# Layer 0 of a two-layer graph network on one Trainium2 core: seven quads a pair instead of eight, features loaded once

## What is computed

```python
edge_index = jnp.stack([src, dst])
row, col = (edge_index[0], edge_index[1])
tp = fctp_messages(node_features[col], edge_attr_tensor, W1, W2, W3, W4)   # bilinear in node (160) and edge (32) features
messages = tp @ Wm + bm
agg = jax.ops.segment_sum(messages, row, num_segments=N_NODES)
```

## Time and profile before

| | us |
|---|---|
| median of 3 runs (2830.77 to 2832.46) | 2830.84 |
| the profiled execution, its own time | 2835.33 |
| its span in the trace | 2833.5 |
| the message loop in it, first pair to last scatter | 65 to 1295 |
| one chunk in it, rank to rank | 25.05 |

### The profile page before, as it was taken

One profiled execution on the slowest core, in us unless ns is written; L12 is line 12 of the kernel. 1 busy time (PEld: TensorE's weight loads), 2 busy tenths in 40 slices (PEclk: granted clock), 3 DMA queues, 4 the chain that ended last, 5 costly groups with the idle time before them and its releaser, 6 DMA issues. The chain is left out here.

```text
span 2833.5 us, 54044 instructions
## 1 busy us (share of the span) xinstructions
PE 2614.8 (92%) x16778; PEld 2330.6 (82%) x16778; DVE 1979.4 (70%) x5259; ACT 852.2 (30%) x2319; POOL 1662.2 (59%) x1770
## 2 busy tenths in 40 slices
PE   4999999999999999996999968999999999998997
PEld 2888788888888888886999958988888888888886
DVE  7677567766667767663777856766777676667766
ACT  2444344444444444431222212222222222222221
POOL 1666566666666666662100017777777777777775
PEclk8999999999999999998999979999999999999999
DMA  6899999999888999865888845333333333333332
GB/s 232 294 314 314 299 319 316 319 324 320 290 290 287 291 300 294 294 215 187 279 279 280 284 141 149 90 86 88 100 86 90 86 101 88 86 88 99 87 88 68
DMA packets 433880, 584.01 MB, mean 206 GB/s; under 512 B 75752, under 2 KB 372409, under 8 KB 421002
## 3 DMA queue, kind: packets, MB, share of 16 engines
q10 hardware_dynamic: 237795, 282.85, 30.4%
q0 software_dynamic: 84144, 149.09, 17.9%
q1 hardware_dynamic: 111656, 148.48, 16.3%
HBM read 352.08 MB, written 228.11 MB: 205 GB/s over the span
## 5 line engine op out<-in xcount | busy, mean ns | idle before, releaser
L444 POOL DMA_INDIRECT placed<-message,slots_now x784 | 762.9, 973 | 486.5 <-ACT message L613 326.6
L1429 POOL DMA_INDIRECT f_y<-y_table,b_rec x894 | 855.4, 957 | 289.6 <-issue 181.9
L528 PEld LDWEIGHTS g_bank<-quad_ring,front_work 128*128 128x128 f32 x6272 | 878.5, 191 | 98.9 <-issue 96.5
L528 PE MATMUL g_bank<-quad_ring,front_work 128*128 x6272 | 942.1, 304 | 8.0 <-DMA quad_ring<-products 7.5
L772 DVE SCALAR_TENSOR_TENSOR front_work<-g_bank,quarter_node,front_work 128x512 f32<-128x512 f32 x784 | 529.6, 743 | 44.2 <-PE g_bank L505 31.8
L1619 PE MATMUL e_bank<-f_msg,f_hot 128*126 128x160 f32 x1788 | 387.6, 312 | 71.7 <-DVE f_msg L1493 70.6
L1490 DVE TENSOR_TENSOR f_msg<-e_bank,f_y 128x256 f32<-128x256 f32 x447 | 189.2, 423 | 319.7 <-issue 223.9
L1614 PE MATMUL e_bank<-f_msg,f_hot 128*126 128x160 f32 x1788 | 395.8, 303 | 18.0 <-DVE f_msg L1493 15.3
L1619 PEld LDWEIGHTS e_bank<-f_msg,f_hot 128*126 128x126 f32 x1788 | 282.0, 189 | 122.9 <-DVE f_msg L1493 121.4
L1602 PE MATMUL e_bank<-fc,b_hidden 100*128 100x192 f32 x1788 | 372.0, 330 | 0.0
L613 ACT COPY message<-g_bank 128x320 f32<-128x320 f32 x392 | 167.2, 427 | 561.9 <-PE g_bank L528 561.9
(11 more groups left out here) (237 smaller groups left out, 2622.7 us busy)
## 6 DMA issues: line engine op xcount, KB each, us to landing
products<-g ACTq DMA_DIRECT2D x49, 2560.0 KB
quad_ring<-products ACTq DMA_DIRECT2D x98, 1280.0 KB
big<-placed SPq DMA_DIRECT2D x49, 1458.0 KB, 7.1
front_work<-in_e_t SPq DMA_DIRECT2D x392, 64.0 KB
b_lengths<-length_parts ACTq DMA_DIRECT2D x447, 45.0 KB
placed<-zeros SPq DMA_DIRECT2D x24, 648.0 KB
f_y<-y_table,b_rec POOLq DMA_INDIRECT x894
placed<-message,slots_now POOLq DMA_INDIRECT x784
```

The source lines that it names most:

```text
L444: pool.indirect_dma_start(v.placed[:, :], bass.IndirectOffsetOnAxis(slots_now[tile // SET % SLOT_SETS][:, tile % SET:tile % SET + 1], 0), ...
L528: last = pe.matmul(bank_now[:, n * D:n * D + D], spread[batch % SPREADS][:, j, q * P:q * P + P], ring[:, bass.ds(slot + j, 1), :].rearrang ...
L1429: pool.indirect_dma_start(f_y[:, tile % Y_RING, :], None, v.y_table[:, :], bass.IndirectOffsetOnAxis(b_rec[b % REC_RING][:, j, 0:1], 0)).t ...
```

## The change

**A joint quad.** A tile needs its fourth quad only where its last node lies more than 11 above its base. Now each tile has three matmuls of its own, and the pair has one more for the tile of the two that needs a fourth (the first, where neither does): seven instead of eight. Its weights are one 128x128 matrix, its quad and its output column (0 or 160) come from registers. VectorE builds three matrices of 128x512 and two of 128x128 a batch instead of four of 128x512. A pair in which both tiles need a fourth quad is added to the violations.

**Words.** A batch has six entries in `places` instead of four: four words (a tile's place and, 8 bits up, the joint place or column) and, for VectorE, the two numbers that say which tile's edges the joint matrix takes. TensorE takes the words apart in registers; VectorE reads its two once a batch. `positions` is longer by ten small steps.

**Features.** One transfer of 32 partitions a batch instead of two; ScalarE copies three quarters (three copies of 32x512) instead of one half (one of 64x512).

```diff
-                    for n in range(2):
-                        sp.dma_start(features[h][32 * n:32 * n + 32, :, :].rearrange("p a b -> p (a b)"), t["e32_t"][:, edges]).then_inc(edges_in[h], 16)
+                    sp.dma_start(features[h][0:32, :, :].rearrange("p a b -> p (a b)"), t["e32_t"][:, edges]).then_inc(edges_in[h], 16)
...
                     for n in range(2):
                         q = pair % 2 * 2 + n
-                        slot = places[batch][q]
-                        for j in range(WINDOW):
-                            last = pe.matmul(bank_now[:, n * D:n * D + D], spread[batch % SPREADS][:, j, q * P:q * P + P],
-                                             ring[:, bass.ds(slot + j, 1), :].rearrange("p a b -> p (a b)"), start=(j == 0), stop=(j == WINDOW - 1))
-                    last.then_inc(expanded, 1)
+                        slot = nc.s_assert_within(words[batch][q] & (2 ** FIELD - 1), 0, RING_QUADS - 1, skip_runtime_bounds_check_because=OF_RING)
+                        for j in range(WINDOW - 1):
+                            pe.matmul(bank_now[:, n * D:n * D + D], spread[batch % SPREADS][:, j, q * P:q * P + P],
+                                      ring[:, bass.ds(slot + j, 1), :].rearrange("p a b -> p (a b)"), start=(n == 0 and j == 0), stop=False)
+                    m = pair % 2
+                    slot = nc.s_assert_within(words[batch][2 * m] >> FIELD, 0, RING_QUADS + WRAP - 1, skip_runtime_bounds_check_because=OF_RING)
+                    column = nc.s_assert_within(words[batch][2 * m + 1] >> FIELD, 0, D, skip_runtime_bounds_check_because=OF_RING)
+                    pe.matmul(bank_now[:, bass.ds(column, D)], spread[batch % SPREADS][:, WINDOW - 1, m * P:m * P + P],
+                              ring[:, bass.ds(slot, 1), :].rearrange("p a b -> p (a b)"), start=False, stop=True).then_inc(expanded, 1)
...
-                    act.copy(features[h][64:128, :, :], features[h][0:64, :, :]).then_inc(features_doubled, 1)
+                    for n in range(1, 4):
+                        last = act.copy(features[h][32 * n:32 * n + 32, :, :], features[h][0:32, :, :])
+                    last.then_inc(features_spread, 1)
...
-                    for j in range(WINDOW):
-                        last = dve.scalar_tensor_tensor(spread[batch % SPREADS][:, j, :], p_node[h % 2][:], v.quarter_node[:, j:j + 1],
-                                                        features[h].rearrange("p a b -> p (a b)"), ALU.is_equal, ALU.mult)
+                    flat = features[h].rearrange("p a b -> p (a b)")
+                    longer = nc.values_load_multi_w_load_instructions(
+                        v.places[:, ENTRY * batch + BATCH:ENTRY * batch + ENTRY], [mybir.EngineType.DVE], min_val=0, max_val=P,
+                        skip_runtime_bounds_check_because="a tile's first edge in its pair is 0 or P")[1]
+                    for j in range(WINDOW - 1):
+                        dve.scalar_tensor_tensor(spread[batch % SPREADS][:, j, :], p_node[h % 2][:], v.quarter_node[:, j:j + 1], flat, ALU.is_equal, ALU.mult)
+                    for m in range(2):
+                        edges = bass.ds(longer[m] + 2 * P * m, P)
+                        last = dve.scalar_tensor_tensor(spread[batch % SPREADS][:, WINDOW - 1, m * P:m * P + P], p_node[h % 2][:, edges],
+                                                        v.quarter_node[:, WINDOW - 1:WINDOW], flat[:, edges], ALU.is_equal, ALU.mult)
```

More of the change, by code:

```diff
@@ L23 @@
 BATCHES = TILES // BATCH
+ENTRY = 6
+FIELD = 8
 PAIRS = TILES // 2
@@ L182, in build_program @@
         v.quarter_node = sb("quarter_node", [P, WINDOW])
-        v.places = sb("places", [1, TILES], I32)
+        v.places = sb("places", [1, BATCHES * ENTRY], I32)
         v.scattered_order = sb("scattered_order", [1, 1], I32)
@@ L260, in front_phase @@
         excess = sb("excess", [P, 2])
+        entry = sb("entry", [CHUNKS, CHUNK // BATCH, ENTRY], I32)
+        long = sb("long", [CHUNKS, CHUNK])
+        fourth = sb("fourth", [CHUNKS, 4, CHUNK // 2])
         small = sb("small", [CHUNKS, 8, CHUNK])
@@ L460, in _, with load_words @@
             def _(pe):
-                places = {}
-                def load_places(batch):
+                words = {}
+                OF_RING = "a place is a quad between 0 and UNITS * UNIT less the ring's laps before it, a column 0 or D"
+                def load_words(batch):
                     if batch >= BATCHES:
                         return
-                    places[batch] = nc.values_load_multi_w_load_instructions(
-                        v.places[:, BATCH * batch:BATCH * batch + BATCH], [mybir.EngineType.PE], min_val=0, max_val=RING_QUADS - 1,
-                        skip_runtime_bounds_check_because="a place is a quad between 0 and UNITS * UNIT less the ring's laps before it")[1]
+                    words[batch] = nc.values_load_multi_w_load_instructions(
+                        v.places[:, ENTRY * batch:ENTRY * batch + BATCH], [mybir.EngineType.PE], min_val=0, max_val=2 ** 17 - 1,
+                        skip_runtime_bounds_check_because="a word is a place and, FIELD bits up, a place or a column")[1]
                 def unit(b, j):
@@ L501, in spread_ids @@
                     batch, h = pair // 2, pair // 2 % 4
-                    pe.wait_ge(edges_in[h], batch // 4 * 48 + 48)
+                    pe.wait_ge(edges_in[h], batch // 4 * 32 + 32)
                     if batch >= 2:
@@ L519, in expand @@
                     if pair % 2 == 1:
-                        load_places(batch + 1)
+                        load_words(batch + 1)
                     pe.wait_ge(built, batch + 1)
@@ L614, in copy_pair @@
                     if pair % 2 == 1:
-                        double_features(pair // 2 + 4)
+                        spread_features(pair // 2 + 4)
                     if k % 4 == 3:
@@ L629, in _ @@
                 for batch in range(4):
-                    double_features(batch)
+                    spread_features(batch)
                 act.wait_ge(ones_set, 1)
@@ L680, in misfits @@
                     tables.link(dve.tensor_tensor(small[:, 7, :], small[:, 5, :], small[:, 6, :], ALU.add))
+                    of_pair = long[:].rearrange("c (p q) -> c p q", q=2)
+                    tables.link(dve.tensor_tensor(fourth[:, 2, :], of_pair[:, :, 0], of_pair[:, :, 1], ALU.mult))
+                    tables.link(dve.tensor_reduce(fourth[:, 3, 0:1], fourth[:, 2, :], AX.X, ALU.add))
                     tables.link(dve.tensor_reduce(chunk[:, 0:1], small[:, 7, :], AX.X, ALU.add))
+                    tables.link(dve.tensor_tensor(chunk[:, 0:1], chunk[:, 0:1], fourth[:, 3, 0:1], ALU.add))
                 def block_starts():
```

35 lines of the change are left out of this document (26 added, 9 removed).

## The result

The changed kernel takes 2804.4 us in the median of four runs (2802.05 to 2805.29), the kernel before 2830.81: a ratio of 0.9905, 95% interval 0.9893 to 0.9917. It saves 26 us and not 83. The profiled execution took 2805.29 us, its span is 2803.6.

What follows compares the result with a forecast made beforehand. TensorE was taken to set the pace, with the DMA engines nearest behind. Gain 100.1 us less 3.3 (start) and 14 (DMA) is 82.8; off the 2830.84 us median that gives 2748 us, 8-in-10 range 2732 to 2785.

Steps and rivals of the forecast that it cites:

- TensorE, 0.272 us a pair less: Message loop: one matmul (two passes) fewer a pair, 2.18 us a chunk, chunk 22.87 us; extra register instructions cost nothing.
- How many chunks gain: 46 chunks gain 2.18 us each, 100.1 us; the last three gain nothing, GpSimd's scatters end them at 1.275 us steps.
- The start, 3.3 us: Before the loop: VectorE's ten small steps and ScalarE's two more first copies lose 3.3 us, between 1.2 and 5.
- The loads of the words: Register loads in the loop: VectorE's new one 0.3 us a batch, hidden; TensorE's 0.35 us, hidden behind queued matmuls.
- the forecast 3 to 4.5: Sign in the loop: VectorE's wait before `held` falls from 6.55 us a chunk to 3 to 4.5 us.
- The rival that had a register load as bound: VectorE's load at the head of each build sets the pace, kernel slower, up to 2924 us; chance 0.04.
- ScalarE's copies at nothing: Loop: eight more copies a chunk, 4.9 us, covered by ScalarE's 11.8 us of waiting for TensorE; cost nothing.
- The sign that I named: Waits on `copied` or on ScalarE's feature copies would show the ScalarE term, costed at nothing, to be wrong.
- The DMA, 14 us: Ring loads lag shorter chunks: 0.5 us lost in each of the first 25, 0.1 in 21 others; bounds nothing to 62.
- my own test (chunks of both halves equal): Sign: equal chunks in both halves would refute the DMA term, which expected 23.2 to 23.6 us before 800 us, 22.9 after.
- the 10 to 20 that I named as a sign: Sign in the loop: TensorE waits on `quad_ring` 10 to 20 us in all, in place of 7.5.
- Its case, 2734: First rival: the DMA costs nothing more in the loop, so the kernel takes 2734 us; chance 0.15.

Runs made afterwards that it cites:

- aligned_products_first: Changed kernel with eight-word entries, four-word aligned loads, and ScalarE's feature copies behind the products' issue: 2778.6 us, 0.9797 (repeat, `_again`); 1.0108 on the 3199.7 us chip.
- before_new_features: Kernel before with only the features' part: one 64 KB transfer a batch, three 32x512 ScalarE copies; 1.0012 on the 3199.7 us chip, repeat 2836.8 us, 1.0003.

## Why the prediction was wrong

The range ended at 2785; the time is 2804. By its own steps:

- **TensorE, 0.272 us a pair less: right.** With both stalls gone the rank matmuls above are 22.98 and 22.95 us apart (22.87 forecast). So the two more register instructions a pair, costed at nothing, cost about 0.1 us a chunk at most.
- **How many chunks gain: as forecast.** GpSimd ends the phase with its last 48 scatters 1.275 us apart (answer to the earlier trace rows):

```profile
1211.13 0.96 POOL L448 DMA_INDIRECT placed<-message,slots_now  x1 [5.35 <-ACT message L624]
...
1271.06 0.97 POOL L448 DMA_INDIRECT placed<-message,slots_now  x1 [0.30 <-issue]
```

- **The start, 3.3 us: about right.** The matmul of ids after VectorE's first build stands at 68.39 against 64.28, 4.1 us later, and the count that the first rank matmul waits for 1.9 us later (44.24 against 42.35):

```profile
44.24 0.66 PE L499 MATMUL g_bank<-r_count,before 128*128 128x49 f32 x2 [9.84 <-DVE r_count L761]
...
62.91 7.56 ACT L613 COPY front_work<-front_work 32x512 f32<-32x512 f32 x12 [8.55 <-issue]
...
68.39 0.58 PE L510 MATMUL g_bank<-id_rows,ones 1*128 1x512 bf16 x1 [13.96 <-DVE front_work L810]
```

- **The loads of the words: the first step that failed.** I costed VectorE's new load (0.3 us; it takes 0.53, and 1.8 once a chunk) and took TensorE's own at its 0.35 us as before, though the change moves it from 16-byte steps to 24-byte steps. No row of the kernel before has an unaligned load, so its price couldn't be read there; that the load can become long could: it took up to 1.142 us, and its long ones stood once a chunk, right behind an issue of ScalarE. TensorE's load went from 0.93 to 3.7 us there and became a stall of 1.1 us a chunk. VectorE's load is hidden in the main: its wait ahead of `held` is still 4.50 us, at the upper end of the forecast 3 to 4.5 (answer to the earlier trace rows). The rival that had a register load as bound had the wrong engine.

```profile
639.08 0.21 DVE L776 TENSOR_TENSOR held<-held,r_count 128x49 f32<-128x49 f32 x1 [4.50 <-PE g_bank L500]
```

- **ScalarE's copies at nothing: the second.** The sum asked whether ScalarE was busy and whether the pair's message came first. It didn't ask what stood behind the copies: the products' issue, with the odd ring load queued behind it. The copies set that issue back by 1.26 us. The sign that I named, waits on `copied` or on its feature copies, could not show it; a part of the delay comes back 16 us later as a wait for a ring load.
- **The DMA, 14 us: a mechanism half right, and too small.** A ring load "of the second kind" was named with its four pairs, but how near it was to being late was read from 7.5 us of waits in all, not from the 1.6 to 2.1 us to spare that landing times show. By my own test (chunks of both halves equal) the term was not what held the changed kernel. Its 14.7 us of waits on `quad_ring` lie in the 10 to 20 that I named as a sign, but that is luck: they are what the stall behind the load left over, and 54.0 us without it. Once both stalls are gone something of the kind is there: mean chunks of 24.41 and 23.12 us are 1.54 and 0.25 over 22.87, and 1.54 x 25 + 0.25 x 21 = 44 us instead of 14. Some 9 us of it are in the kernel before too, whose mean chunk is 25.42 in the first half, and most of that lies in two chunks: chunks 8 and 9, counted from 0, take 27.3 and 30.1 us there, and 26.0 and 30.6 in aligned_products_first_again. SyncE sends `block_start` at that place (L429, at 282.8 us); whether that is the cause wasn't tried.
- **The sum by the loop's length.** Before, the loop's first to last scatter takes 1223.4 us (the earlier trace rows has its end), after 1196.2: 27.1 less. In aligned_products_first_again it is 1160.6, 62.8 less. So of the 86.1 that I expected of the loop (100.1 - 14), 35.7 went into the two stalls and 23.3 more are missing even without them. I put those beside the DMA term, whose cause stays open.
- **The Trainium skill's rule** ("DMA: Bandwidth & Descriptors", Specifications: some 358 GB/s of HBM for a core) would have made the DMA term nothing. Its case, 2734, didn't come either. The row that I set against it (319 GB/s at a share of 1.00) shows no ceiling though: a window of the changed kernel reaches 399.

```profile
444.00:448.40 4.40, 4.40 (x33) 4.00 (x32) 3.36 (x8) 2.43 (x6) 2.68 (x4) 1.00 1.03 399
```

Another page of the Trainium skill ("HBM Reference", Specifications (TRN2)) says that a core which streams alone gets well above that share; by that, the trace agrees.

## What to carry to other kernels

Cost a change of a table's layout at every engine that reads it into registers: in these runs the cheapest load was one of four words from a multiple of 16 bytes. Of a step that is put on an engine, ask what DMA issue stands behind it, and follow that transfer to the one who needs it; the landing time against the first use gives the slack, which no busy share does. Where taking away one stall brings nothing, look for a second in the same stretch before giving the first one up: the version with aligned entries and the copies behind the products saves 58 us, where the change as it was and each of the two mends alone save 18 to 26. The same holds for what seems to be worth nothing: the single transfer of features seemed to be worth 7 us beside one stall, and its lack goes with 0.9 to 1.0 us a chunk where that stall is gone.

## What the runs showed of the hardware

- ScalarE's copy of 32x512 takes 616 ns, as long as one of 64x512 (617).
- The gain depends on the chip: aligned_products_first is 0.9797 of the kernel before on one chip and 1.0108 (1.0079 to 1.0137) on one where TensorE is granted less. There the granted clock in this stretch of the loop is 0.96, lower than the 1.00 of a kernel with all its matmuls on the same chip (before_new_features), which takes 1.0012:

```profile
500.00:700.00 200.00, 183.77 (x1028) 149.60 (x1027) 133.13 (x295) 111.31 (x257) 122.88 (x124) 0.96 0.92 293
```

```profile
500.00:700.00 200.00, 195.16 (x1175) 162.52 (x1174) 133.34 (x257) 113.69 (x263) 122.80 (x125) 1.00 0.89 297
```

In the loop of aligned_products_first TensorE has 51 waits called "issue" there, 50.1 us in all; in the long ones its sequencer shows no instruction until some 0.3 us before the end. What causes them wasn't found.
